# Two-layer cross-attention on one core: transposed token scores with a row of maxima, sums by a product with ones, and units in other slots

## What is computed

```
ca_q1  = einsum('btc,th->bch', ca, Wq_ca)[:, indices, :]   # 112 rows
ca_hs1 = _mha(ca_q1, residual, residual)                   # 8 heads, 112 x 112 scores
ca_q2  = ca_hs1 @ Wq
ca_hs2 = _mha(ca_q2, ca @ Wk_ca, ca @ Wv_ca)               # 4 keys
out    = (hs + ca_hs2) @ Wout + b_out + residual
```

## Time and profile before

| | us |
|---|---|
| median of 3 runs | 844.62 |
| lowest, highest | 840.89, 852.93 |
| the profiled execution | 842.08 |
| its span in the trace | 840.3 |
| TensorE busy with matmuls in the span | 744.2 |
| VectorE busy | 473.5 |
| ScalarE busy | 396.8 |
| GpSimd busy | 292.1 |

### The profile page before, as it was taken

One profiled execution on the slowest core, in us unless ns is written; L12 is line 12 of the kernel. 1 busy time (PEld: TensorE's weight loads), 2 busy tenths in 40 slices (PEclk: granted clock), 3 DMA queues, 4 the chain that ended last, 5 costly groups with the idle time before them and its releaser, 6 DMA issues.

```text
span 840.3 us, 18167 instructions
## 1 busy us (share of the span) xinstructions
PE 744.2 (89%) x6920; PEld 637.1 (76%) x6920; DVE 473.5 (56%) x1027; ACT 396.8 (47%) x922; POOL 292.1 (35%) x401
## 2 busy tenths in 40 slices
...
GB/s 302 94 92 174 46 143 44 111 64 94 89 58 136 31 141 52 83 92 70 112 37 150 37 110 65 99 84 60 133 30 128 62 84 83 54 111 9 69 8 8
...
## 3 DMA queue, kind: packets, MB, share of 16 engines
...
q10 hardware_dynamic: 896, 0.20, 0.1%
...
## 4 chain that ended last, share of the span: by engine, by line
PE 57%; DVE 18%; ACT 15%; issue 4%; DMA 3%; ACTq 2%; SPq 0%; POOL 0%; DVEq 0%; POOLq 0%
PE bankX L972 22%; PE bankO L1192 9%; DVE negmax L758 6%; PE bankST L1160 6%; ACT arena L572 4%; PE bankS L1126 4%; ACT arena L554 3%; PE bankST L1154 3%; PE bankX L1038 2%; DVE q1T L814 2%; PE bankS L1123 2%; DVE negmax L822 2%; PE bankX L1092 2%; DVE stage L799 2%; ACT stage L602 2%
## 5 line engine op out<-in xcount | busy, mean ns | idle before, releaser
L758 DVE TENSOR_REDUCE negmax<-bankS 112x2 f32<-112x750 f32 (+1 forms) x224 | 208.7, 932 | 70.3 <-PE bankS L1126 38.5
L478 POOL DMA_DIRECT2D k_stack<-stage x192 | 96.2, 509 | 161.2 <-DVE stage L794 136.9
L1192 PE MATMUL bankO<-arena,v 125*32 125x112 f32 (+2 forms) x2688 | 120.0, 278 | 6.7 <-ACT arena L554 5.6
L554 ACT ACTIVATE arena<-bankST 125x1344 f32<-125x1344 f32 x80 | 103.5, 1293 | 33.0 <-PE bankST L1160 33.0
L1192 PEld LDWEIGHTS bankO<-arena,v 125*32 125x32 f32 (+2 forms) x2688 | 91.9, 126 | 30.8 <-issue 16.7
L1126 PE MATMUL bankS<-k_stack,q1T 112*112 112x376 f32 x320 | 91.6, 369 | 4.9 <-DVE negmax L758 4.9
L972 PE MATMUL bankX<-ctx_hi,WH 128*120 128x376 f32 (+2 forms) x192 | 75.9, 395 | 2.8 <-DVE qn L750 2.6
L572 ACT ACTIVATE arena<-bankX,negmax 112x112 f32<-112x112 f32 x128 | 43.5, 352 | 60.6 <-DVE negmax L822 60.6
L1160 PE MATMUL bankST<-q1T,k_stack 112*125 112x224 f32 x480 | 69.3, 281 | 2.3 <-DMA q1T<-mT 2.2
L972 PE MATMUL bankX<-ctx_hi,WL 128*120 128x376 f32 (+2 forms) x192 | 67.9, 353 | 0.0
L972 PE MATMUL bankX<-WH,ctx_hi 128*125 128x320 f32 x192 | 65.6, 342 | 1.1 <-ACT v L609 0.6
...
## 6 DMA issues: line engine op xcount, KB each, us to landing
...
k_stack<-stage SPq DMA_DIRECT2D x192, 70.5 KB, 4.0
k_stack<-stage POOLq DMA_DIRECT2D x192, 47.0 KB, 3.5
...
```

The costliest lines, as they stand in the source:

```text
L478: pool.dma_start(dst, src).then_inc(k1_stacked_pool[b % 2], 16)
L554: nc.scalar.activation(dst[0:KC], bankST[0:KC, :, 0:GROUP * SQ], ACT.Exp).then_inc(exp_done, 1)
L758: nc.vector.tensor_reduce(negmax[:, n % 2, 2 * pair:2 * pair + 2], bankS[0:SQ, :, 0:keys], axis=AX, op=ALU.max, negate=True).then_inc(max_ ...
L1192: last = nc.tensor.matmul(dst, v, src[0:keys, c, SQ * j:SQ * j + SQ], start=(c == 0), stop=(c == NKC - 1))
```

## The change

- The softmax of the tokens' attention is now computed like the large ones. S2 is scored as before, DVE takes the row maxima (now the bank's only reader), TensorE transposes the maxima (new unit M2), DVE copies them to m2T, and a DMA on SP's queue (`place_m2`) puts them as row 96 into `cabd`. The scores are computed a second time, transposed and shifted (new unit S2T, with w2s, which has a row of ones added, as weights, and cabd as the moving side). cabd is the token matrix spread over heads by POOL (`expand_ca`). ACT takes two exponentials of 448 columns straight into prob2T.
- exps2, the sums, reciprocal2, normalise2, T2 and the copy after PV2 are gone.
- A new unit Z2 multiplies a 112x64 matrix of ones with prob2T, in two matmuls of 448 columns, one for each half of the columns. So each row of hs1T has its sum in every row. DVE inverts all of Z2 (128x448) and multiplies PV2 with it; this is the drain of PV2's bank.
- The units stand in other slots (below). K1_1 and K1_2 move from slot 2 to slots 5 and 6, so stack_k1 for batch t-1 is issued in iteration t. normalise3 and split_p3 move to slot 4. V0_1 and V0_2 run in the batch's own iteration.
- On POOL, stack_k1 now stands behind expand_w2 and ahead of split_ctx. On SP it stands first in the iteration, and place_m2 stands behind load_ctx.
- MT_BUFS goes from 4 to 2.

```diff
-    ([("K1_1", 0)], [("S3", 0)], [("N1b", -2), ("S2_0", 1)], [("K1_2", 0)]),
-    ([("S2_1", 1)], [("K0_0", 1)], [("hn1T", -2), ("q0T_0", 1)], [("K0_1", 1)]),
+    ([("q1T_1", -1)], [("q1T_2", -1), ("N1b", -2)], [("M2", 1), ("q0", 1)], [("PV2", 0), ("Z2", 0), ("K1_0", 0)]),
+    ([("K0_0", 1)], [("hn1T", -2)], [("K0_1", 1)], [("S3", 0), ("S2T_0", 1)]),
...
+            def place_m2(b):
+                if b > 0:
+                    sp.wait_ge(unit_filled, filled("S2T_1", b - 1))
+                sp.wait_ge(bank_drained[bank("M2", b)], drained("M2", b))
+                sp.dma_start(cabd[96:97, :, :].bitcast(F32), m2T[:, :].bitcast(F32).unsqueeze(1))\
+                    .then_inc(m2_placed, 16)
...
-            def normalise2(b):
-                pool.wait_ge(rsum2_done, b + 1)
-                pool.wait_ge(w2_expanded if b == 0 else ctx_split, b + 1)
-                nc.gpsimd.tensor_tensor(prob2[0:SQ], prob2[0:SQ],
-                                        rsum2[:, :].unsqueeze(2).broadcast_to((SQ, H0, SQ)),
-                                        ALU.mult).then_inc(prob2_ready, 1)
+            def expand_ca(b):
+                pool.wait_ge(ca_split, b + 1)
+                pool.wait_ge(x_split, b + 1)
+                pool.wait_ge(ctx_split, max(b, 1))
+                if b > 0:
+                    pool.wait_ge(unit_filled, filled("S2T_1", b - 1))
+                nc.gpsimd.tensor_tensor(
+                    cabd[0:96, :, :], ca_st[:, :].bitcast(F32).unsqueeze(1).broadcast_to((96, H0, SQ)),
+                    mask96.unsqueeze(2).broadcast_to((96, H0, SQ)), ALU.mult).then_inc(ca_expanded, 1)
...
                 if t + 1 < B:
                     expand_w2(t + 1)
-                    split_ctx(t + 1)
...
-                if t < B:
-                    stack_k1(t, range(4, 8))
+                if 0 <= t - 1 < B:
+                    stack_k1(t - 1, range(4, 8))
                 if t + 1 < B:
-                    normalise2(t + 1)
+                    split_ctx(t + 1)
+                if t + 2 < B:
+                    split_ca(t + 2)
+                    split_x(t + 2)
+                    expand_ca(t + 2)
...
-            def exps2(b, half):
-                act.wait_ge(max2_done, 2 * b + half + 1)
-                X = bankX[bank(f"S2_{half}", b)]
-                for h in range(4 * half, 4 * half + 4):
-                    last = nc.scalar.activation(prob2[0:SQ, h, :], X[0:SQ, (h % 4) * SQ:(h % 4 + 1) * SQ], ACT.Exp,
-                                                bias=negmax2[:, h:h + 1], accum_out=sum2[:, h:h + 1])
...
+                elif kind == "S2T":
+                    if b > 0 and i == 0:
+                        act.wait_ge(unit_filled, filled("Z2", b - 1))
                     nc.scalar.activation(prob2T[0:SQ, 4 * i:4 * i + 4, :].rearrange("p h q -> p (h q)"),
-                                         X[0:SQ, 0:4 * SQ], ACT.Copy).then_inc(free, 1)
+                                         X[0:SQ, 0:4 * SQ], ACT.Exp).then_inc(free, 1)
...
+                elif kind == "Z2":
+                    dve.wait_ge(unit_filled, filled(name, b))
+                    sums = hs1T.rearrange("p c q -> p (c q)")
+                    nc.vector.reciprocal(sums, X[:, 0:4 * SQ]).then_inc(free, 1)
+                    dve.wait_ge(free, drained(name, b))
+                    nc.vector.tensor_tensor(sums, bankX[bank("PV2", b)][:, 0:4 * SQ], sums, ALU.mult)\
+                        .then_inc(bank_drained[bank("PV2", b)], 1)
...
+                elif kind == "S2T":
...
+                    last = nc.tensor.matmul(X[0:SQ, 0:4 * SQ], w2s[:, :],
+                                            cabd[:, 4 * i:4 * i + 4, :].rearrange("p h q -> p (h q)"), start=True,
+                                            stop=True)
...
+                elif kind == "Z2":
+                    if b == 0:
+                        pe.wait_ge(w2_ones, 2)
+                    for odd in range(2):
+                        last = nc.tensor.matmul(X[64 * odd:64 * odd + 64, 0:4 * SQ], ones2[:, :],
+                                                prob2T[0:SQ, odd:H0:2, :], start=True, stop=True)
```

More of the change, by code:

```diff
@@ L40 @@
 DMAS_K0, DMAS_K1 = 9, 12
-MT_BUFS = 4
+MT_BUFS = 2
 UNITS = [
[7 rows of a table removed]
[7 rows of a table added]
 ]
 PHASES = range(4)
-FIRST_UNITS = ["W2", "q0", "K0_0", "K0_1", "K0_2", "S2_0", "S2_1", "q0T_0", "q0T_1", "T2_0", "T2_1",
-               "V0_0", "V0_1", "V0_2"]
+FIRST_UNITS = ["W2", "q0", "K0_0", "K0_1", "K0_2", "S2_0", "S2_1", "M2", "q0T_0", "q0T_1", "S2T_0", "S2T_1", "V0_0"]
 ITERATIONS = range(0, B + 2)
@@ L363, in _ @@
             load_x(1)
+            place_m2(0)
             stack_k0(0, range(3))
@@ L370, in _ @@
             for t in ITERATIONS:
+                if 0 <= t - 1 < B:
+                    stack_k1(t - 1, range(4))
                 if t < B:
@@ L380, in _ @@
                     load_ctx(t + 2)
-                if t < B:
-                    stack_k1(t, range(4))
                 if t + 1 < B:
+                    place_m2(t + 1)
+                    stack_k0(t + 1, range(3))
                     load_xp(t + 1)
-                if t + 1 < B:
-                    stack_k0(t + 1, range(3))
                 if 0 <= t - 2:
@@ L485, in _ @@
             expand_w2(0)
+            expand_ca(0)
             for tile in (k0_stack, *k1_stack):
                 nc.gpsimd.memset(tile[:, :, :].bitcast(F32), 1.0).then_inc(zeroed, 1)
-            normalise2(0)
             add_bias0(0)
@@ L491, in _ @@
             split_x(1)
-            pool.wait_ge(x_split, 2)
+            expand_ca(1)
+            pool.wait_ge(ca_expanded, 2)
             nc.gpsimd.memset(odd_rows[:, :], 1.0).then_inc(q1T_zeroed, 1)
@@ L580, in unit @@
                 i = int(i or 0)
-                if kind in ("out0", "out1", "N0", "N1a", "N1b"):
-                    return
-                if kind == "S2":
-                    exps2(b, i)
+                if kind in ("out0", "out1", "N0", "N1a", "N1b", "S2", "M2", "PV2", "Z2"):
                     return
                 if kind == "S3":
-                    act.wait_ge(bank_drained[bank("S3", b)], drained("S3", b))
+                    act.wait_ge(free, drained(name, b))
                     nc.scalar.activation(p3[:, :, :], p3[:, :, :], ACT.Exp).then_inc(exp3_done, 1)
@@ L679, in _ @@
             round_weights(2)
-            unit("T2_0", 0)
-            unit("T2_1", 0)
+            unit("S2T_0", 0)
+            unit("S2T_1", 0)
             round_weights(3)
@@ L685, in _ @@
                 round_g(m)
-            for i in range(3):
-                unit(f"V0_{i}", 0)
+            unit("V0_0", 0)
             for t in ITERATIONS:
```

94 lines of the change are left out of this document (44 added, 50 removed), and 10 rows, old and new, of the table UNITS.

## The result

The changed kernel takes 981.69 us (median of 4 runs, 974.71 to 987.63), beside 845.25 us (840.89 to 852.93) for the kernel before in the same rounds: a ratio of 1.16, 95% interval 1.149 to 1.171, slower. The forecast was 955 us with a range of 885 to 1000 and 0.88 on slower. The profiled execution of the changed kernel took 974.71 us, with a span of 972.5.

The account below looks back on a forecast made before the run. The prediction took TensorE's own work plus one bad place, slot 3, as the bound. Its terms summed to +6.8 us a batch, 109 in 16, plus 4 at the end: 842.1 + 109 + 4 = 955 us, range 885 to 1000.

Parts of the forecast that it names:

- The slot 3 gap: Slot 3: TensorE's idle before hn1T and q0T_0, behind ACT's small exponentials, goes; -3.0 us a batch.
- TensorE's work: TensorE: S2T, M2 and Z2 come and T2 goes; +1.1 us a batch, bounds 0.9 to 1.9.
- K1_0's wait: Slot 2: K1_0 waits for PV2's bank while DVE inverts and multiplies 448 columns; +3.8 us a batch, bounds 1.4 and 6.5.
- M2 and q0: Slot 2: M2 waits 1.7 behind q1T_2's drains, q0 0.4 for N1b's bank; +2.1 us a batch, bounds 0.8 and 2.6.
- The K-stack wait: Start of slot 2: layer 1's scores wait for the stack's DMAs behind expand_w2; +1.6 us a batch, bounds 0 and 4.
- Other bank waits: q0T_1, S2T_0, q0T_0 and V1_1 wait for banks, less some old small idle; +1.2 us a batch, bounds 0 and 2.5.
- Clock: TensorE's clock: the same slow stretch follows K1_0's longer gap; 0 us a batch, bounds -1.5 and +1.5.
- heavier: Rival: reciprocal at 8 to 9 ns an element and a second clock fall (+1.5); +9.4 a batch, 996 us; chance 0.15.
- The end: Last iteration: slots 0 and 1 nearly empty, SP's 12 DMAs and their landing late by some 4 us; +4 in all.
- quick reciprocal: Rival: DVE's reciprocal takes 0.6 us, K1_0 waits 1.45, the clock stays up; +3.0 a batch, 893 us; chance 0.09.
- Not slower: Rival: K1_0 waits under about 1.5 us, clock kept; 823 us, or 849 with the stack wait; chance 0.10.
- Work removed from ACT pays elsewhere: Rival: TensorE's small waits for ACT, at most 0.90 us in the first window, come back; 940 us; within the forecast's 0.66.

Follow-up runs that it names:

- e6: e5 with VectorE's reciprocal replaced by a copy of the same shape, so the normalisation is left out; 833.21 us, ratio 0.988.
- e8: e7 with PV2 and Z2 copied out of their banks by ACT, the inversion in four pieces and some units moved; 817.05 us, ratio 0.968.
- e1: Changed kernel with VectorE's reciprocal of Z2 replaced by a copy of the same shape, normalisation left out; 904.63 us, ratio 1.069.
- e4: Changed kernel with split_ctx of batch 1 ahead of the clearing of v1 at the start; 976.41 us, ratio 1.151.
- e5: Changed kernel with the edits of e2, e3 and e4 together; 905.90 us, ratio 1.071.
- e7: The new attention in the slots and GpSimd and SyncE queues of the kernel before, with place_m2 and expand_ca added; 891.54 us, ratio 1.056.
- e2: Changed kernel with the K stack's DMAs on GpSimd issued ahead of expand_w2; 928.04 us, ratio 1.094.
- e3: Changed kernel with q1T_1 and q1T_2 back in slot 1; 916.52 us, ratio 1.082.

## Why the prediction was right, and where its sizes were off

The sign, the place and the main cause were right, and the time lay in the range. That the batch came out within 0.5 us of the forecast is partly luck, since two terms were off in opposite directions. Step by step:

- **The slot 3 gap, -3.0: right.** hn1T's wait for ACT's small exponentials and q0T_0's for K0_0's drain are gone. This gain is real, and e6 and e8 keep it.
- **TensorE's work, +1.1: right.** Z2 takes 0.93 for 4 records of 448 columns (1.1 was taken, because its order was held to allow less overlap), so its halves overlap like PV2's, 0.94. S2T_0 is one matmul with 0.29 between its start and the next: 463.55 to 463.84. With 0.6, 0.93 and 0.1 against T2's 0.7 the sum is 0.9.

```profile
463.55 0.46 PE L1094 MATMUL bankX<-cabd,w2s 97*112 97x448 f32 x1 [0.15 <-DVE stage L801]
463.84 0.51 PE L1142 MATMUL bankS<-k_stack,q1T 112*112 112x376 f32 x2
```

- **K1_0's wait, +3.8: right, 3.72.** The reciprocal takes 2958 ns and the product 624. The two small reciprocals were the right pair: between 112 elements (844 ns) and 448 the slope is (2958 - 844) / 336 = 6.29 ns an element, where the forecast read 6.25 off 4 and 16. The other pair, 12.5 ns an element, rested on the 8-element row of 148, and that row is the odd one: in the changed kernel 4, 8 and 16 elements take 174, 201 and 258. By the repeat count of 8 in the Trainium skill, "VectorE: DVE Perf Modes" (section "First, the fixed hardware budget"), the reciprocal was an estimate of 3.7 us, and by the cycle table of that page (section on the TRN2 errata) an estimate of 0.59; the measured 2.96 agrees with neither. VectorE is busy 540.2 us in all, where about 530 was named. The wait as a cause is shown by e1.
- **M2 and q0, +2.1: too large.** M2 waits 1.40 in the three iterations that keep the clock and 0.76 in the others, where 1.7 was taken. Before q0 the timeline shows no wait of TensorE's matmuls, where 0.4 was taken. When the clock is low TensorE itself comes later to M2, and so waits less there. No run took M2's wait away alone.
- **The K-stack wait, +1.6: right, 1.9 on average,** from 1.04 to 2.81. From expand_w2's start to the scores it is 441.88 - 431.21 = 10.7 us; the forecast's 12.6 - 1.85 is 10.75.
- **Other bank waits, +1.2: too large.** q0T_1 waits 0.47 and the others 0.15 to 0.27, 1.1 a batch in all where small waits were 0.9 before, so some 0.2 was added.
- **Clock, 0: this is the term that failed.** The waits together were sized at 5.7 us a batch (3.8 + 2.1 + 1.6 + 1.2 less 3.0), and idle grew by only 3.6. Busy time, sized at 1.1, grew by 3.7. The 2.8 that is neither idle nor work is the lower clock. The step behind it read: the new gap is longer than the one that goes, so the same slow stretch follows. In fact slot 2 idles at three places, and in 9 of 12 iterations the clock fell at or behind the first, the stack wait (0.69 over 16.1 us in the one shown). The rival "heavier" had this second fall, and its +1.5 for it was nearer than the forecast's 0. The waits were taken 2.1 too high and the work 0.2, the clock 2.8 too low; this nearly cancels, so 6.8 was forecast and 7.3 measured.
- **The end, +4: the wrong end, and too small.** The tail grew by 2.2; the head grew by 20.5. The timeline of the changed kernel shows in it:

```profile
68.51 1.70 POOL L528 MEMSET v<- 128x1920 f32 x1 [18.76 <-DMA g_rows<-v]
68.58 0.60 PE L975 MATMUL bankX<-ctx_hi,WH 128*128 128x376 f32 x1 [3.72 <-DVE arena L842]
...
75.93 0.64 PE L975 MATMUL bankX<-ctx_hi,WH 128*120 128x376 f32 x1 [5.50 <-POOL ctx_hi L446]
```

K1_0's wait comes once here too, and K0_0 of the next batch waits 5.50 for split_ctx, which on GpSimd stands behind a clearing that itself waits for DMAs. The forecast counted 6.8 for this stretch, as for a batch. Up to the first out0 TensorE is busy 68.8 of 96.3 us at a granted clock of 0.77, where before it was 59.8 of 75.8 at 0.91: of the 20.5, 9.0 are busy time and 11.5 idle. K1_0's 3.72, K0_0's 5.50, and the first wait for the DMA of q0T's row, 2.05 where it was 0.70, make 10.6 of the idle part. The first out0 is 4.0 earlier in e4 and 11.7 earlier in e5; how much of that is the edits' own is not shown.

Of the rivals, the quick reciprocal fell with the 2958 ns. "Not slower" fell with K1_0's 3.72, but e6 bears out its reasoning: with K1_0 at 1.38 and the orders mended the clock is kept, and the time is 1.2% below the kernel before, though without the normalisation. "Work removed from ACT pays elsewhere" is not seen in the changed kernel: ACT fell to 347.4 us busy, and its small waits are 1.1 us a batch where they were 0.9.

What the runs show of the whole: most of the loss is the slots with their queue orders (90 us by e7), less the new attention in the old slots (46). The two buffers for mT in place of four were not varied; VectorE's copies into mT sat idle 48.7 us in the changed kernel, 47.4 of them for TensorE's transpose, so they leave little room for a cost. Single repairs overlap and are not to be added: e2, e3 and e4 alone gain 54 + 65 + 5 = 124 and together 76, while the copy gains 77 with the bad orders in place and 73 without. All eight stack waits of 1.45 us or more went with a lower clock in slot 2, and one of the four shorter ones; what decides between those four stays open.
